# Rotary attention with its operands on strips of 32 partitions instead of stacks of 99 rows

## The reference

```python
# 16 heads of 8 dims, T = 2048, causal
qkv = x @ W_qkv.T ; q, k = rope(q), rope(k)
scores = q @ k.T / sqrt(8), masked where key > query
o = softmax(scores) @ v ; x = x + o @ W_out.T
```

## Time and profile before

| what | us |
|---|---|
| median of 3 runs (lowest, highest) | 1947.14 (1944.35, 1948.87) |
| the profiled execution: span, first to last instruction | 1933.1 |
| rotary stage, first projection to the last chunk's output | 370.9 to 937 |
| PE busy over the span | 1601.7 (83%) |
| DVE busy over the span | 1180.5 (61%) |
| ACT busy, POOL busy | 786.5, 818.4 |

### The profile page before, as it was taken

The page is one execution under the profiler, slowest core; times in us unless marked ns, Lnnn a source line. Parts: engine busy times, 40 slices in busy tenths (PEclk is TensorE's granted clock), DMA queues, the critical chain, the costliest instruction groups (busy, mean ns, idle before and its releaser), DMA issues.

```text
span 1933.1 us, 25832 instructions
## 1 busy us (share of the span) xinstructions
PE 1601.7 (83%) x8863; PEld 807.4 (42%) x8863; DVE 1180.5 (61%) x2315; ACT 786.5 (41%) x1031; POOL 818.4 (42%) x987
## 2 busy tenths in 40 slices
PE   4766699758999899999799789989545898988779
PEld 2222466412333333332466567766212333333256
DVE  5887633578788787883333333342355878897951
ACT  2222233343565565667333344444212343334433
POOL 2224646464554635455463644000001577456900
PEclk8788699867999999999799999979656898889979
DMA  4000000151000303000000000000143000000000
GB/s 139 1 0 0 1 1 0 59 121 29 2 2 12 41 3 51 2 2 1 1 1 0 0 1 0 0 1 0 49 117 96 1 1 1 1 1 1 1 1 22
DMA packets 31585, 36.86 MB, mean 19 GB/s; under 512 B 8606, under 2 KB 24703, under 8 KB 31362
## 3 DMA queue, kind: packets, MB, share of 16 engines
q1 hardware_dynamic: 27906, 29.29, 6.4%
q10 hardware_dynamic: 3520, 6.29, 1.6%
q0 software_dynamic: 64, 0.00, 0.0%
HBM read 26.10 MB, written 8.91 MB: 18 GB/s over the span
## 4 chain that ended last, share of the span: by engine, by line
PE 61%; DVE 16%; DMA 7%; SPq 3%; issue 2%; ACT 2%; ACTq 0%; DVEq 0%
PE PS L943 9%; PE PS L1355 9%; PE PS L931 9%; PE PS L1304 8%; PE PS L1374 8%; DVE sb_latent_acc L1462 3%; DMA sb_rope_K<-rope_parts 3%; PE PS L1723 3%; PE PS L1741 3%; SPq L1629 2%; DVE sb_latent_mp L1538 2%; DMA latent_parts<-sb_latent_parts 2%; DVE sb_rope_mp L1538 2%; DVE sb_latent_rec L1568 1%; PE PS L1735 1%
## 5 line engine op out<-in xcount | busy, mean ns | idle before, releaser
L1538 DVE TENSOR_REDUCE sb_rope_mp<-PS 128x1 f32<-128x512 f32 (+3 forms) x560 | 345.0, 669 | 76.5 <-PE PS L1308 36.9
L1418 ACT ACTIVATE sb_rope_PT<-PS 128x1024 f32<-128x1024 f32 (+3 forms) x320 | 273.3, 895 | 223.0 <-PE PS L1359 121.7
L1462 POOL TENSOR_TENSOR sb_latent_acc<-sb_latent_acc,sb_latent_PT 128x1536 f32<-128x1536 f32 (+3 forms) x72 | 223.2, 3101 | 72.4 <-ACT sb_latent_PT L1418 68.8
L1418 ACT ACTIVATE sb_latent_PT<-PS 128x1024 f32<-128x1024 f32 (+3 forms) x160 | 140.2, 895 | 243.3 <-PE PS L1359 80.9
L995 DVE SCALAR_TENSOR_TENSOR sb_X<-PS,sb_gates,sb_X 128x128 f32 (+1 forms) x320 | 90.1, 344 | 241.3 <-PE PS L943 241.2
L1304 PE MATMUL PS<-sb_rope_K,sb_rope_Q 96*128 96x512 bf16 (+3 forms) x640 | 211.7, 371 | 30.2 <-ACT sb_rope_V L1399 18.3
L1538 DVE TENSOR_REDUCE sb_latent_mp<-PS 128x1 f32<-128x512 f32 (+3 forms) x280 | 174.3, 666 | 46.2 <-PE PS L1304 32.5
L576 POOL TENSOR_SCALAR sb_pbelow<-sb_pa,sb_ptrial 128x512 f32<-128x512 f32 x124 | 197.0, 1599 | 6.4
L583 POOL TENSOR_TENSOR sb_pbelow<-sb_pbelow 128x1024 f32<-128x1024 f32 (+1 forms) x248 | 181.7, 733 | 19.6
L931 PE MATMUL PS<-sb_HT,sb_w 128*128 (+1 forms) x384 | 182.3, 612 | 3.6 <-DVE sb_seed L514 1.9
L1355 PE MATMUL PS<-sb_rope_Q,sb_rope_K 99*128 99x512 bf16 (+3 forms) x640 | 179.4, 352 | 1.4 <-ACT sb_rope_PT L1418 0.9
(11 more groups left out here) (291 smaller groups left out, 2438.7 us busy)
## 6 DMA issues: line engine op xcount, KB each, us to landing
latent_parts<-sb_latent_parts SPq DMA_DIRECT2D x36, 128.0 KB
sb_rope_Q<-rope_parts SPq DMA_DIRECT2D x9, 384.0 KB
rope_parts<-sb_rope_parts SPq DMA_DIRECT2D x24, 128.0 KB, 2.4
sb_rope_tab<-in_rotation SPq DMA_DIRECT2D x1, 2048.0 KB, 8.6
sb_rope_K<-rope_parts SPq DMA_DIRECT2D x6, 256.0 KB
sb_latent_Q<-latent_parts ACTq DMA_DIRECT2D x2, 768.0 KB
sb_latent_Q<-latent_parts SPq DMA_DIRECT2D x1, 1536.0 KB, 19.1
sb_rope_Q<-rope_parts ACTq DMA_DIRECT2D x6, 192.0 KB
```

The lines of the kernel that those rows point to most:

```text
L1418: s.activation(self.PT[:, u % 2, 2 * p:2 * p + 2, q0:CH], k.PS[:, 2 * p:2 * p + 2, q0:CH], ACT.Exp, scale=self.scale).then_inc(self.exps[p ...
L1462: eng.tensor_tensor(acc, acc, new, ALU.add).then_inc(self.added[who], 1)
L1538: v.tensor_reduce(self.mp[:, n % 2, kc, heads[0]:heads[-1] + 1, i], k.PS[:, bank, 0:len(heads) * w].rearrange("p (h k) -> p h k", h=len(he ...
```

## The change

`rope_attention` uses a new class, `RopeStrips(Strips)`. The latent attention still uses `CausalHeads`; a class `LatentStrips` is added and never built. What the new stage does:

- Each head of a quad lies on its own strip of 32 partitions, 24 of them used. Two operand pairs, A and B, hold three products of parts each: `QA`, `KA`, `QB`, `KB`, all four quads in SBUF at once. A score or maximum block is now two matmuls of 32 rows (A, then B), where it was one of 96 or 99. The negated maximum sits in spare rows of B.
- The strips are built on PE from the parts, by matmuls with 0/1 matrices (`select`, a new input, loaded and rounded at setup). ACT copies three operands out of PSUM, DVE the fourth. There is no DRAM scratch, and the stacks' DMAs, the constants' writes and the four DMAs per chunk for the negated maxima are gone. The rotation table comes in four pieces.
- The opening (`opening`) works on four banks at a time and includes the maxima of the first two chunks. The loop starts when all of it is done.
- The chunks go in another order: chunk 0 of quads 0 and 1, chunks 1 and 2 of quad 0, chunk 3 of all four quads, then what is left of 2, 1 and 0.
- Per unit the plan has `scores` of one pair, two maximum blocks of the other two strips, `weighted` of the unit before, `scores` of the second pair, two blocks of the first two strips, then the rest. The waits for the two ring banks and the masks stand ahead of the scores.
- `PT` is three units deep. Each loop maximum block has a bank and a reduction of its own, also where it is narrow. 608 blocks are in the loop: 8 at unit 0, 6 at units 1 to 20, 4 at 21 to 128, 2 at 129 to 152, none after.
- A layer norm can be told which tiles are left; after this stage they are tiles 0 to 3.

```diff
+class Strips(Stage):
+    R = 3
+    AHEAD = 3
+    PTS = 3
...
+        for c in [0, 0] + list(range(1, NC - 1)) + [NC - 1] * nq + \
+                [c for c in range(NC - 2, 0, -1) for _ in range(nq - 1)] + [0] * (nq - 2):
+            seq.append((c, left[c].pop(0)))
...
+        for u in range(total):
+            want = max([np.ceil((d - done) / max(1, at - u) / 2) * 2 for at, d, _ in due if d > done] or [0])
...
+        for u in range(total + 12):
+            mine = steps[u]
+            pairs = (0, 1) if not mine or mine[0][4] == 2 else (1, 0)
+            if u < total:
+                plan.append((u, f"scores{pairs[0]}"))
+                plan += ring(mine[0:2])
+            if 1 <= u <= total:
+                plan.append((u - 1, "weighted"))
+            if u < total:
+                plan.append((u, f"scores{pairs[1]}"))
+                plan += ring(mine[2:4])
...
+            plan += ring(mine[4:])
+            for it in rests[u]:
+                if it[0] == "turn":
+                    plan.append((u, ("split", it[1])))
+                plan.append((None, it))
...
+    def pe_scores(self, pe, u, p, beside):
...
+        if u:
+            pe.wait_ge(self.exps[p], u)
...
+        self.pe_max_masks(pe, beside)
+        for j in pair:
+            ins = self.pe_head(pe, j, n, kj, q0, not diag)
+        ins.then_inc(self.scores[p], 1)
+        self.pe_maxima(pe, beside)
+    def pe_max_masks(self, pe, items):
+        for ring, (_, n, i, kc, j) in items:
+            b, uses = self.bank_of(ring)
+            if uses:
+                pe.wait_ge(self.ring_free[b], uses)
...
+    def split(self, eng, ch, n, row):
...
+        ch(eng.tensor_copy(part(0), neg))
+        ch(eng.tensor_tensor(rest, neg, part(0), ALU.subtract))
+        ch(eng.tensor_copy(part(1), rest))
+        eng.tensor_tensor(part(2), rest, part(1), ALU.subtract).then_inc(self.neg_split, 1)
...
+        v.tensor_reduce(self.mp[:, n % 2, i, j:j + 1, kc], k.PS[:, bank, 0:w], AX.X, ALU.max) \
+            .then_inc(self.ring_free[b], 1)
...
+class RopeStrips(Strips):
+    PATTERNS = [(0, 1), (2, 3), (0, 2), (1, 3), (0,), (1,)]
+    TERMS = {"QA": ((0, 0), (1, 1)), "KA": ((2, 0), (3, 1)), "QB": ((4, 0), (5, 2)), "KB": ((4, 2), (5, 0))}
...
+        plan.append(new(("project", 2)))
+        step("rotate", 2)
+        quads(0)
+        step("split", 1)
+        selects(1, "QA", "KA", "QB", "KB")
+        plan.append((-1, ("negatives", 0)))
...
+        return plan + [(None, ("turn", 0)), (None, ("turn", 1))]
...
+            for t in range(2):
+                for g in range(4):
+                    ins = self.pe_select(pe, c, g, op, t, bank + g, t == 1)
...
+    def pe_head(self, pe, j, n, kj, q0, start):
...
+        pe.matmul(k.PS[:, j, q0:CH], self.KA[strip, g, kj * P:(kj + 1) * P],
+                  self.QA[strip, g, c * CH + q0:(c + 1) * CH], start=start, stop=False, skip_group_check=True)
+        return pe.matmul(k.PS[:, j, q0:CH], self.KB[strip, g, kj * P:(kj + 1) * P], self.QN[strip, n % 2, q0:CH],
+                         start=False, stop=True, skip_group_check=True)
...
+        if kind == "turn":
+            pe.matmul(k.bank(bank), k.identb[:, :], self.QB[:, g, c * CH:(c + 1) * CH], start=True, stop=False,
+                      skip_group_check=True)
+            pe.wait_ge(self.neg_split, n + 1)
+            for i in range(TPC):
+                ins = pe.matmul(k.PS[:, bank, i * P:(i + 1) * P], self.negp[:, n % 2, i, :], k.identb[:, :],
+                                start=False, stop=True, skip_group_check=True)
...
+                    s.activation(self.QN[:, n % 2, :], k.PS[:, 5 + b, :], ACT.Copy).then_inc(self.ring_free[b], 1)
...
-            a = CausalHeads(k, "rope", ln, 4, [(k.wqkvT[:, i, :], k.wqkvT[:, 3 + i, :]) for i in range(2)],
...
+            a = RopeStrips(k, "rope", ln, [(k.wqkvT[:, i, :], k.wqkvT[:, 3 + i, :]) for i in range(2)],
+                           k.wqkvT[:, 2, :], k.woutT, d["rotation"])
```

More of the change, by code:

```diff
@@ L37, with left_tiles @@
     tiles_ahead = 0
+    def left_tiles(self):
+        return self.tiles_ahead, NT - self.tiles_ahead
     def sync(self, sp):
@@ L105, in __init__ @@
         self.eps = sb("eps", [P, 1])
+        self.select = sb("select", [P, len(RopeStrips.PATTERNS), P], BF16)
+        self.neg_rows = self.cst[:, CST_ORDER + 8:CST_ORDER + 9]
         self.PS = ctx.enter_context(nc.psum_tensor("PS", [P, 8, CH], F32))
@@ L191, in __init__ @@
         self.ready = self.mem.ready
-        self.ahead = 0
+        self.left = (0, NT)
     def statistics(self, v, n, tiles):
@@ L212, in vector @@
                 v.wait_ge(sem, val)
-        self.statistics(v, self.ahead, NT - self.ahead)
+        self.statistics(v, *self.left)
         for n in range(NT):
-            v.wait_ge(m.steps, first + n + 1)
+            v.wait_ge(m.steps, first + (n + 1 if self.left[0] + self.left[1] == NT else NT))
             ins = v.bn_aggr(m.mv[:, n, :], m.stats[:, n, :])
@@ L307, in alloc @@
         self.wo = sb("wo", [P, 8, P])
+        self.selection = sb("selection", [P, len(RopeStrips.PATTERNS), P])
         self.row0 = sb("row0", [3, 8, P])
@@ L355, in loads @@
         load(k.wkv[:, 1, :], d["L1_attn_b_wv_down"])
+        load(self.selection[:, :, :], d["selection"])
         return early, out
@@ L440, in gpsimd @@
         g.tensor_copy(k.identb[:, :], k.ident).then_inc(self.ready, 1)
+        g.tensor_copy(k.select[:, :, :], s.selection[:, :, :]).then_inc(self.ready, 1)
         g.tensor_copy(k.mask_qk[:, :], k.cst[:, (5 + 8) * P:(6 + 8) * P]).then_inc(self.ready, 1)
@@ L447, in tensor @@
         pe.wait_ge(s.ready, 1)
-        pe.wait_ge(self.ready, 4)
+        pe.wait_ge(self.ready, 5)
         n = 0
@@ L1863 @@
 CST_ORDER = N_CST * P
-CST_COLS = N_CST * P + 8
+CST_COLS = N_CST * P + 9
 def constants():
@@ L1881, in constants, with selection @@
     c[:, 14 * P:15 * P] = np.where(r[:, None] > r[None, :], MASKED, 0.0)
-    c[:, CST_ORDER:] = 8 - np.arange(8)
+    c[:, CST_ORDER:CST_ORDER + 8] = 8 - np.arange(8)
+    c[:, CST_ORDER + 8] = (r % 32 >= RopeStrips.NEG_ROW) & (r % 32 < RopeStrips.NEG_ROW + 3)
+    return c
+def selection():
+    c = np.zeros((P, len(RopeStrips.PATTERNS), P), np.float32)
+    r = np.arange(P)
+    for i, blocks in enumerate(RopeStrips.PATTERNS):
+        for b in blocks:
+            c[r, i, 32 * (r % 32 // 8) + 8 * b + r % 8] = 1.0
     return c
@@ L1917, in norm @@
                 if producer.tiles_ahead:
-                    producer.next_ln, ln.ahead = ln, producer.tiles_ahead
+                    producer.next_ln, ln.left = ln, producer.left_tiles()
                     break
```

718 lines of the change are left out of this document (714 added, 4 removed).

## The result

The changed kernel takes 2095.32 us (median of 4 runs, 2093.20 to 2107.76) against 1945.74 us: ratio 1.0798, 95% interval 1.0741 to 1.0856. It is slower by 150 us. The forecast was slower by 75, at 2022.

What follows compares the result with a forecast made beforehand. PE was taken to bound the loop before; with the change it waits for banks. The loop's 66 us more plus the prologue's 9 made 75, so 1933.1 became 2008, with 14.0 to the median 2022; range 1900 to 2160.

Steps and rivals of the forecast that it cites:

- The ring's waits: Main loop: scores groups wait for two of three maximum-block banks, so a four-block unit takes 3.04 us against 2.82.
- s: Main loop, time for heads issued ahead of a group's blocks: taken as 0.07 us, with 0.03 to 0.22 possible.
- rival 1: Main loop: PE keeps strict program order among strips, loop pairs take 553 us instead of 424, total 2159; chance 0.20.
- Prologue 95: Before the loop: the DRAM trip goes, a chain of ACT, DVE and PE replaces it; 95 us against 86.
- Chunk ends: Main loop, 14 turns: PE waits about 2.2 us for DVE's split; 3.0 us each, 42 in all.
- rival 2: Main loop: PE's idle gaps put a third of the time at 1.2 GHz, 55 us more, total 2077; chance 0.13.
- the three signs of being wrong: Main loop: DVE busy over 90%, four-block units under 2.8 us, or granted clock under 0.9.
- Units 129 to 159: End of the loop: exponent, weighted product, second scores, exponent in series, 2.75 us at full width; 69 us in all.
- rival 3: Main loop: banks come free earlier and DVE becomes the bound, loop 421 us, total 1899; chance 0.18.
- Units 21 to 128: Middle part of the loop: 356 us in the forecast's sum, nine chunk ends of 3.0 us included.
- The range for this case alone: Whole kernel: 1990 to 2085, from s (-11 to +42), chunk ends (-14 to +28) and the prologue's ends.
- Span to median: Whole kernel: 14.0 us taken to lie between profiled span and median, added to 2008 to give 2022.

Runs made afterwards that it cites:

- a_then_b: The changed kernel with first passes of a group's two heads and two blocks all ahead of the second passes; 2103.74 us, ratio 1.0851.
- fill3: The changed kernel with three zero-weight 512-column matmuls more per unit, after the second scores group and its blocks; 2060.59 us, ratio 1.0624.
- no_swap: The changed kernel with the pair of heads 0 and 1 always first in a unit; 2065.46 us, ratio 1.0676.
- short_reduce: The changed kernel with each maximum-block reduction reading 128 columns, not up to 512, leaving out part of the maximum; 2022.02 us, ratio 1.0444.
- ns_turn_fill: The changed kernel with heads 0 and 1 always first, the turn one unit after DVE's split, and three zero matmuls after each unit's second group; 2041.17 us.
- wa_short: The changed kernel with the weighted product behind both scores groups and reductions reading 128 columns; 1982.06 us, ratio 1.0206.

## Why the prediction was right in direction and wrong in size

- **The ring's waits, a full unit of 3.04**: right. 3.07 was measured in the unit shown, 3.14 in the median. Strips run side by side with s near 0.02 for the first passes; the handoff to DVE is 0.07, not 0.04.
- **Strict order (rival 1)**: false, by the timeline and by a_then_b. The Trainium skill (TensorE: Matmul & The Clock Gate, Part 3, "The mechanism") says that matmuls start and end in program order. The first head's second pass stands ahead of the second head's first pass in the program; the trace has them at 703.30 and 703.08. The measurement decides.
- **Prologue 95, first scores at 466, tail 11**: right. 94 to the first exponent, the first scores at 462, and 12.
- **Chunk ends 14 x 3.0, with 2.2 of it PE's wait**: about right for eleven of them, whose waits are 1.6 to 2.9 us, 23.7 in all. At the last three PE waits 0.5 in all, and the gap of 4 us that was to be the sign came nowhere. The time at 1.2 GHz was not priced: at six of the nine turns of the middle part a stretch of it starts within 1.5 us of the turn.
- **The clock (rival 2, 2077, chance 0.13)**: this failed. The forecast kept the clock of before and put its loss at nothing. Of the three signs of being wrong, "under 0.9" is the one that came. Measured 0.83, the very figure of the rival. fill3 gives 40 us for it, 19 of them in units 0 to 20, where the earlier trace rows had no stretch to compare. Of two stretches in the earlier trace rows, 36 us with gaps at 1.00 was trusted over 30 us with gaps at 0.83; nothing in them said which the new loop, with 0.9 us of gap per unit and 2.4 at turns, would be like.
- **Units 129 to 159 at 2.75 us full width, 69 in all and 78 with their chunk ends**: this failed too, by 37 us. The chain of exponent, weighted product, second scores and exponent has the right members, but it was given a wrong start: I let the first scores group of a unit wait for nothing. With the order of the pairs alternating it waits for the exponent just issued. 3.64 us came at full width instead of 2.75 (mask of 0.2 included), PE idled, and part of the time went to 1.2 GHz. no_swap gives back 32 of the 37.
- **Faster at 1899 (rival 3)**: false. DVE isn't the next bound behind the ring; the exponent's chain of 2.87 to 3.08 is (short_reduce).
- **Units 21 to 128, 28 us over**: at a clock of 0.98 fill3 still has 19 of them. A median unit of 3.14 instead of 3.04 would be 11, an estimate. With the turns' waits gone too (ns_turn_fill) the part takes 364 us, where the forecast less nine waits of 2.2 would be 336. So 8 to 17 us at least are not explained.
- **The range for this case alone, 1990 to 2085**: its own terms don't add up to it. 2022 + 42 + 28 + 10 is 2102 at the high end. The measured 2095 lies between the two, but for a reason that none of these terms has.
- **Span to median, 14.0**: this term was misread, as said above; 1.9 us lie outside the span.
- The stages behind take 1004 us for 996 (clock 0.83 for 0.84 in the last 670 us). No run here asked why.

## What to carry to other kernels

When an edit turns PE from the bound into an engine that waits, price its gaps twice: once as waits, once as time at the lower clock, and look for the places where gaps are longest, not at the mean. Where a plan changes the order of two alternating buffers from step to step, write down for each step which exponent or reduction its first instruction needs; the swap is one short line in the diff, and without it units 129 to 159 took 32 us less. And before a wait is called the bound, work out the next chain behind it: here, in the units followed, the two differed by 0.2 us, and cutting one alone gave 73 us where 195 to 245 were expected.

## What the runs showed of the hardware

- Three matmuls of 512 columns with zero weights per unit, 0.65 us together, placed where PE waits, raise the granted clock of the loop from 0.83 to 0.96 and make it 40 us shorter (fill3).
- Eight 512-column passes on four row strips end within 0.62 us of their common start (703.08 to 703.70), 2.8 times faster than eight passes of 0.22 in a row would be (1.76).
- PE goes on 0.44 us after DVE's start on a reduction of 128 columns (705.05 to 705.49 in wa_short, 0.28 of it the reduction) and 0.84 after one of 512 columns (705.31 to 706.15 in the changed kernel, 0.68 of it the reduction): 0.16 for the handoff in both.
